# Perceiver block on one core: tokens split by context quarter, output weights in the key weights' buffer, last weighings in four banks

## What is computed

```python
x = x + xattn(layernorm(x), ctx)      # q = x Wq; k, v = ctx Wk, ctx Wv
                                      # softmax(q k / sqrt(32)) v, then @ Wp + bp
x = x + attn(layernorm(x))            # q, k, v, o with biases, per-head bias on the keys
x = x + ffn(layernorm(x))             # relu(x W_fc)^2 W_proj, five spiking steps, mean of spikes
```

## Time and profile before

| | us |
|---|---|
| median of 3 runs (lowest, highest) | 1918.98 (1917.98, 1925.94) |
| the profiled execution | 1919.2 |
| its span | 1917.4 |
| PE busy in the span | 1849.8 (96%) |
| DVE, POOL, ACT busy | 1116.4, 873.9, 834.6 |
| mean granted PE clock | 0.987 of 2.4 GHz |

### The profile page before, as it was taken

One profiled execution on the slowest core, in us unless ns is written; L12 is line 12 of the kernel. 1 busy time (PEld: TensorE's weight loads), 2 busy tenths in 40 slices (PEclk: granted clock), 3 DMA queues, 4 the chain that ended last, 5 costly groups with the idle time before them and its releaser, 6 DMA issues. The chain is left out here.

```text
span 1917.4 us, 65530 instructions
## 1 busy us (share of the span) xinstructions
PE 1849.8 (96%) x28992; PEld 1595.3 (83%) x28992; DVE 1116.4 (58%) x1354; ACT 834.6 (44%) x1032; POOL 873.9 (46%) x830
## 2 busy tenths in 40 slices
PE   6999999999999999999999999999999989789998
PEld 3979898989888888888888989898989768667887
DVE  4475665657474848384848474747475561763265
ACT  4444444545453535353535353545444413334322
POOL 0293636454554546372728282828272620544211
PEclk9999999999999999999999999999999989789999
DMA  5200202011010202020202020202020140222110
GB/s 211 85 4 3 76 3 76 16 64 45 34 68 12 77 2 77 3 77 3 76 3 76 3 76 3 76 3 76 3 75 3 67 133 23 46 72 91 52 56 23
DMA packets 38829, 94.54 MB, mean 49 GB/s; under 512 B 18593, under 2 KB 18593, under 8 KB 38305
## 3 DMA queue, kind: packets, MB, share of 16 engines
q1 hardware_dynamic: 38560, 90.26, 13.3%
HBM read 81.99 MB, written 6.16 MB: 46 GB/s over the span
## 5 line engine op out<-in xcount | busy, mean ns | idle before, releaser
L379 POOL TENSOR_TENSOR fold<-fold,prob 128x256 f32<-128x256 f32 (+1 forms) x704 | 700.3, 995 | 55.2
L98 PE MATMUL ring<-y_parts,wk_s 128*128 128x402 f32 (+1 forms) x3072 | 607.4, 351 | 1.4 <-PEq L152 1.4
L98 PE MATMUL ring<-wv_s,y_parts 128*128 128x512 f32 (+1 forms) x2496 | 596.2, 396 | 0.0
L98 PEld LDWEIGHTS ring<-y_parts,wk_s 128*128 128x128 f32 x3072 | 551.1, 188 | 17.4 <-issue 4.1
L98 PEld LDWEIGHTS ring<-wv_s,y_parts 128*128 128x128 f32 (+1 forms) x2496 | 453.8, 184 | 112.6
L373 POOL TENSOR_TENSOR fold<-prob 128x256 f32<-128x256 f32 x64 | 68.2, 1066 | 698.0 <-ACT prob L416 698.0
L393 ACT ACTIVATE k_sb<-ring 128x402 f32<-128x402 f32 (+1 forms) x256 | 129.4, 505 | 372.5 <-PE ring L98 372.5
L525 DVE TENSOR_TENSOR prob<-prob,peak_rows 128x1024 f32<-128x1024 f32 (+1 forms) x192 | 277.9, 1499 | 12.2 <-ACT peak_rows L412 12.2
L406 ACT ACTIVATE prob<-s_ps 128x1536 f32<-128x1536 f32 (+1 forms) x128 | 199.9, 1561 | 128.0 <-PE s_ps L642 128.0
L416 ACT ACTIVATE prob<-prob 128x1024 f32<-128x1024 f32 (+1 forms) x192 | 207.5, 1123 | 3.2 <-DVE prob L525 1.3
L502 DVE TENSOR_TENSOR fold<-prob 128x512 f32<-128x512 f32 x64 | 51.8, 809 | 228.2 <-ACT prob L406 228.2
(11 more groups left out here) (142 smaller groups left out, 1474.7 us busy)
## 6 DMA issues: line engine op xcount, KB each, us to landing
y_raw<-yT SPq DMA_DIRECT2D x48, 804.0 KB, 5.8
y_raw<-yT SPq DMA_DIRECT2D x16, 792.0 KB, 9.9
f_raw<-w_ffn SPq DMA_DIRECT2D x22, 512.0 KB, 3.2
p_x<-x SPq DMA_DIRECT2D x2, 1024.0 KB, 7.2
q_scratch<-p_x SPq DMA_DIRECT2D x4, 512.0 KB, 2.7
q_sb<-q_scratch SPq DMA_DIRECT2D x16, 128.0 KB, 8.5
x_sb<-x SPq DMA_DIRECT2D x4, 512.0 KB, 6.1
v_sw<-y_raw SPq DMA_DIRECT2D x4, 512.0 KB, 8.5
```

The lines of the kernel that those rows point to most:

```text
L98: mm = pe.matmul(out, left(a, c), right(b, c), start=(c == 0 and n == 0), stop=(c == DC - 1 and n == 2))
L379: pool.tensor_tensor(acc[0:m], acc[0:m], prob[0:m, i, t, :], ALU.add).then_inc(sum_step, 1)
```

## The change

Four things at the end of cross-attention, and what follows from them in later blocks:

- The parts of the attended tokens are no longer packed over the whole context (`att`) but lie as whole tiles of 128 inside the context's quarters: tiles 0 to 2 at column 0, 3 to 5 at 402, 6 and 7 at 804 (`outputs`, `attended`). So a quarter can be written once the value tiles that read it are done. The stored tokens return in three transfers, and `gather(q)` splits them, on ACT and DVE, inside the last batch's values phase.
- The parts of Wp go to `w_keep`, which is also the key weights' buffer `wk_s` (their last use is before the last values), and now stays for the whole kernel; Wo goes there later too.
- The four last weighings have a bank each: the three of the ring and `small_ps`; PE no longer waits between them. The reciprocals go to four slices of `q_sb`.
- The next block's weights lie in free columns of the context (`w_side`) instead of `awq_s` and `att_room`; `pT` of self-attention lies in `w_raw`; the feed-forward stage has 5 places of its own for weights instead of 7, and two in `w_keep` (`place_of`).

```diff
+TILES = KW // P
+BY_QUARTER = [q * KW for q in range(-(-TT // TILES))]
+TILES_LEFT = TT - TILES * (len(BY_QUARTER) - 1)
...
+        self.keep = ctx.enter_context(nc.sbuf_tensor("w_keep", [P, 2, DC, D], F32R))
-        self.w_out = parts[:, :, DC * TOK:DC * TOK + DC * D].rearrange("p s (c e) -> p s c e", c=DC)
+        side = BY_QUARTER[-1] + TILES_LEFT * P
+        self.w_side = [self.parts[:, :, :, at:at + D] for at in (side, 0, D)]
+    def outputs(self, s, q):
+        return self.parts[:, s, :, BY_QUARTER[q]:BY_QUARTER[q] + tiles_of(q) * P]
+    def attended(self, s, c, t):
+        at = BY_QUARTER[t // TILES] + t % TILES * P
+        return self.parts[:, s, c, at:at + P]
...
-        self.wk_s, self.wv_s = sb("wk_s", [P, 2, DC, D], F32R), sb("wv_s", [P, 2, DC, D], F32R)
+        self.wk_s, self.wv_s = context.keep, sb("wv_s", [P, 2, DC, D], F32R)
...
+        def last_bank(i):
+            return ring[i] if i < RING else small_ps
...
-            sp.dma_start(o_raw[:, :, 0:STORED], o_dram).then_inc(o_back, 16)
+            for q in range(len(BY_QUARTER)):
+                at = stored(q)
+                sp.dma_start(o_raw[:, :, at], o_dram[:, :, at]).then_inc(o_back[q], 16)
...
         @block.scalar
...
+            def gather(q):
+                act.wait_ge(o_back[q], 16)
+                act.wait_ge(full, UNITS * (B - 1) + KEYS + LAST_V[q] + 1)
+                act.activation(stored_part(0, q), o_raw[:, :, stored(q)], ACT.Copy).then_inc(out_hi, 1)
...
                 value(b, 3)
                 if more:
                     high(b + 1, 0)
+                else:
+                    act.wait_ge(wp_in, 16)
+                    act.activation(y.keep[:, 0], y.w_raw, ACT.Copy).then_inc(wp_hi, 1)
                 value(b, 5)
                 peak_row(b, 3)
                 if more:
                     high(b + 1, 1)
+                else:
+                    gather(0)
...
-            act.wait_ge(full, UNITS * B)
-            act.wait_ge(wp_in, 16)
-            act.activation(y.w_out[:, 0], y.w_raw, ACT.Copy).then_inc(out_hi, 1)
-            act.wait_ge(o_back, 16)
-            for c in range(DC):
-                act.activation(y.att[:, 0, c, 0:STORED], o_raw[:, c, 0:STORED], ACT.Copy).then_inc(out_hi, 1)
             act.wait_ge(o_out, NBLK * B)
-            act.activation(y.att[:, 0, :, STORED:TOK], o_sb[:], ACT.Copy).then_inc(out_hi, 1)
+            act.activation(last_part(0), o_sb[:], ACT.Copy).then_inc(out_hi, 1)
...
         @block.vector
...
+            def gather(q):
+                dve.wait_ge(out_hi, q + 1)
+                dve.tensor_tensor(stored_part(1, q), o_raw[:, :, stored(q)], stored_part(0, q).bitcast(F32),
+                                  ALU.subtract)
...
-            dve.wait_ge(out_hi, 1)
-            dve.tensor_tensor(y.w_out[:, 1], y.w_raw, y.w_out[:, 0].bitcast(F32), ALU.subtract)
-            output(B - 1, 0)
-            output(B - 1, 1)
-            output(B - 1, 2)
-            output(B - 1, 3)
-            for c in range(DC):
-                dve.wait_ge(out_hi, 2 + c)
-                dve.tensor_tensor(y.att[:, 1, c, 0:STORED], o_raw[:, c, 0:STORED],
-                                  y.att[:, 0, c, 0:STORED].bitcast(F32), ALU.subtract)
+            output(B - 1, 0, last_bank(0), q_sb[:, 0, :])
+            gather(2)
+            output(B - 1, 1, last_bank(1), q_sb[:, 1, :])
+            output(B - 1, 2, last_bank(2), q_sb[:, 2, :])
+            output(B - 1, 3, last_bank(3), q_sb[:, 3, :])
...
             for i in range(NBLK):
-                if i:
-                    small_output(B - 1, i - 1)
-                weigh(B - 1, i)
+                weigh(B - 1, i, last_bank(i))
...
-    RAW, OWN, HELD, AS, HS, HB = 3, 7, 13, 2, 3, 4
+    RAW, OWN, HELD, AS, HS, HB = 3, 5, 13, 2, 3, 4
+    FREE = OWN + 2
```

More of the change, by code:

```diff
@@ L107, in reached, with tiles_of @@
     eng.wait_ge(sem, count)
+TILES = KW // P
+BY_QUARTER = [q * KW for q in range(-(-TT // TILES))]
+TILES_LEFT = TT - TILES * (len(BY_QUARTER) - 1)
+def tiles_of(q):
+    return TILES if q < len(BY_QUARTER) - 1 else TILES_LEFT
 class Context:
@@ L330, in row, with stored, stored_part, last_part @@
             return peak_rows[:].unsqueeze(1).broadcast_to((P, b - a, HQ))
+        def stored(q):
+            return slice(q * TILES * P, min(q * TILES * P + tiles_of(q) * P, STORED))
+        def stored_part(s, q):
+            return y.outputs(s, q)[:, :, 0:stored(q).stop - stored(q).start]
+        def last_part(s):
+            return y.outputs(s, len(BY_QUARTER) - 1)[:, :, -N:]
         def half_tiles(h):
@@ L462, in values_phase @@
                     high(b + 1, 2)
+                else:
+                    gather(1)
                 value(b, 11)
@@ L525, in subtract, with output @@
                     dve.tensor_tensor(piece(i, n), piece(i, n), row(n), ALU.subtract).then_inc(sub_ok, 1)
[L527 removed]
+            def output(b, i, at=small_ps, share=rec[:]):
                 block = NBLK * b + i
                 dve.wait_ge(pv_ok, block + 1)
[L530 removed]
+                dve.reciprocal(share, at[:, N:2 * N]).then_inc(rec_ok, 1)
                 dve.wait_ge(rec_ok, block + 1)
@@ L571, in values_phase @@
                     low(b + 1, 1)
+                else:
+                    dve.wait_ge(wp_hi, 1)
+                    dve.tensor_tensor(y.keep[:, 1], y.w_raw, y.keep[:, 0].bitcast(F32), ALU.subtract)
                 value(b, 10)
@@ L848, in output_and_qkv @@
         bp_sb, bv_sb, b_col = sb("bp_sb", [P, D]), sb("bv_sb", [P, D]), sb("b_col", [P, 2, NBLK])
-        wq_s = sb("awq_s", [P, 2, DC, D], F32R)
         w_qk = sb("aw_raw", [P, 2, DC, D])
         w_raw = [w_qk[:, 0], w_qk[:, 1], context.w_raw]
-        att_room = [context.att[:, a].rearrange("p c t -> p (c t)").rearrange("p (s c e) -> p s c e", s=2, c=DC)
-                    for a in range(2)]
-        w_s = [wq_s[:], *att_room]
+        w_s = context.w_side
         bank = [ctx.enter_context(nc.psum_tensor(f"co_ps{i}", [P, 512], F32)) for i in range(8)]
-        norm = OutputAndNorm(nc, ctx, "co", context.att, context.w_out, x_sb, xnT, context.rows, ident, bank)
+        norm = OutputAndNorm(nc, ctx, "co", context.attended, context.keep, x_sb, xnT, context.rows, ident, bank)
         x_in, bp_in, b_in, bv_in = [sem(f"x_in{n}") for n in range(4)], sem("bp_in"), sem("b_in"), sem("bv_in")
@@ L914, in _ @@
             act.wait_ge(wo_in, 16)
-            act.activation(context.w_out[:, 0], context.w_raw, ACT.Copy).then_inc(wo_hi, 1)
+            act.activation(context.keep[:, 0], context.w_raw, ACT.Copy).then_inc(wo_hi, 1)
         @block.vector
@@ L940, in _ @@
                     dve.wait_ge(wo_hi, 1)
-                    dve.tensor_tensor(context.w_out[:, 1], context.w_raw, context.w_out[:, 0].bitcast(F32),
+                    dve.tensor_tensor(context.keep[:, 1], context.w_raw, context.keep[:, 0].bitcast(F32),
                                       ALU.subtract)
@@ L1178, in output_and_feed_forward @@
         h_ps, y_ps = bank[:4], bank[4:]
-        norm = OutputAndNorm(nc, ctx, "so", context.att, context.w_out, x_sb, xnT, context.rows, ident, bank)
+        norm = OutputAndNorm(nc, ctx, "so", lambda a, c, t: context.att[:, a, c, t * P:(t + 1) * P], context.keep, x_sb, xnT, context.rows, ident, bank)
         y_sb = context.rows.rearrange("p (t d) -> p t d", t=TT)
@@ L1200, in place_of @@
         def place_of(load):
-            if load % HELD < OWN:
-                return w_own[:, load % HELD]
-            at = (load % HELD - OWN) * 2 * D
-            return context.parts[:].rearrange("p s c m -> p s (c m)")[:, :, at:at + 2 * D]
+            slot = load % HELD
+            if slot < OWN:
+                return w_own[:, slot]
+            if slot < OWN + 6:
+                at = (DC * TOK + (slot - OWN) * 2 * D) % (6 * 2 * D)
+                return context.parts[:].rearrange("p s c m -> p s (c m)")[:, :, at:at + 2 * D]
+            at = (slot - OWN - 6) * 2 * D
+            return context.keep[:].rearrange("p s c e -> p s (c e)")[:, :, at:at + 2 * D]
         def tokens(n):
```

29 lines of the change are left out of this document (15 added, 14 removed).

## The result

| | before | with the change |
|---|---|---|
| median of 9 runs (lowest, highest), us | 1921.0 (1917.09, 1925.94) | 1913.74 (1911.41, 1916.78) |
| the profiled execution, us | 1919.2 | 1911.55 |
| its span, us | 1917.4 | 1909.4 |
| PE busy, us | 1849.8 | 1846.3 |
| mean granted PE clock | 0.987 | 0.989 |

The account below looks back on a forecast made before the run. PE, 96% busy, was taken as the bound, waiting for DVE around the last weighings. 10.5 us (4.1 waits, 2.7 clock, 3.7 tail) plus 1.5 at the next stage made 12.0 off 1919.2: 1907.2 us, range 1903.0 to 1913.5.

Parts of the forecast that it names:

- Weighings in four banks: End of cross-attention: PE's three waits for DVE vanish, fourth weighing ends at 1533.80 us; 4.1 us from waits, 2.7 from clock.
- Full clock in the weighings: Last four weighings: PE's granted clock stays full, worth 2.7 us on the second and third.
- Rival (2): Last weighings run at half clock: 1914.6 us, or 1911.6 with two of four at half speed; chance 0.12.
- The tail: From the fourth weighing's end to the next stage's first product: 2.10 us, a gain of 3.7 us.
- The range: Whole kernel: 1903.0 to 1913.5 us, from gains of 12.4 and 7.6 us with 3 and 2 us of luck.
- The splits beside the values at no cost: Value phase: ACT's and DVE's moved splits fit into gaps ahead of value copies, nothing late; tight ACT gap 0.9 us spare.
- Rivals (3): Value phase: the five split pieces each delay PE by 0.5 us, giving back 2.5 us, 1909.7 us; chance 0.09.
- (4): Value phase: ACT waits for the first quarter's transfer; slower by over 0.5% from a landing at 1532.2; chance 0.02.
- The next stage's start: First 72 products after cross-attention: shorter gap helps the clock; gain 1.0 to 1.9 us, middle 1.5 taken.
- the upper case: Next stage's start: clock stays at 1.00, products end 2.6 us earlier, but DVE limits the gain to 1.9 us.
- The sum of 12.4: Whole kernel's gain in us if the shortened gap keeps full clock into the next stage: 10.5 + 1.9, 1906.8 us.
- Everything else at nothing: Rest of the kernel: three transfers land in time, moved buffers change only addresses; no cost or gain.

Follow-up runs that it names:

- banks alone: The kernel before with a bank for each of the four last weighings, splits still behind the value products; ratio 0.997 to the kernel before.
- the weighings doubled: The changed kernel with the 52 products of each of the last four weighings done twice; 1926.33 us, ratio 1.0024 to the kernel before.
- the splits alone: The changed kernel with the last weighings in one bank again, splits still moved into the value phase; ratio 0.9962 to the kernel before.
- the weighings put between: The changed kernel with the last batch's weighings cut up between value products 7 to 12; ratio 0.9929 to the kernel before, 1911.01 us in the second set.

## Why the prediction was wrong

- **The step that failed** is "1526.93 + 3 x 1.70 + 1.77 = 1533.80 us for the end of the fourth" under *Weighings in four banks*. The 1.70 us was measured on one weighing between large products, where instructions come in while the large ones run. Four in a row took 9.67 us, 2.8 more than the 6.87 of the sum. In its place the runs showed a limit that the sum did not have: PE used up its instructions faster than they came. With banks alone the 2.8 us are there, half of it while no other engine works; with the weighings doubled the stops follow the count of instructions; spread out, they vanish. The waits that the banks removed had been covering part of it, about half by the run with the splits alone.
- **Full clock in the weighings** was right: no row of them is at 0.50. Rival (2), slow weighings, had the direction and a time near the measured one (1911.6 to 1914.6) by a cause that did not occur.
- **The tail** was right to 0.01 us: 2.09 against 2.10. **The range** has a slip of its own: 1919.2 less 12.4 and 3 is 1903.8, not 1903.0. It does not touch the miss, which is at the other end.
- **The splits beside the values at no cost** held: PE's value products run without a stop, and from ACT's peak row to the first weighing it takes 17.61 us as against 17.60 before. Rivals (3) and (4) did not occur; the pieces of the stored tokens landed 8.0 and 9.1 us after their issue. A bound on the way was broken: POOL's totals grew by 5.5 us, not at most the 4.0 of DVE's two-input work. The 4.0 had counted two of DVE's three pieces. By the prediction's own times the third, at 1526.65, began before the bound of 1527.5 and had to be counted; and two of them were longer than worked out. Beside the totals DVE did 2.76 + 1.88 + 1.75 = 6.4 us of it. The totals still ended (1528.6) well before the fourth weighing needed them.
- **The next stage's start** was forecast with 1.5 us between 1.0 and 1.9; 1.03 came. The clock stayed at 1.00 after the gap of 2.09 us, the upper case; the product stretch shrank from 19.51 to 16.90 as worked out, and DVE added the fourth tile at 1550.24, 11.9 us after the stage's first product instead of 14.1. What was gained on the clock was then given back to DVE's small operations: 2.02 us for a pair that had taken 0.36, while the one ahead of it went only from 0.95 to 0.44. That the shorter gap keeps the clock, as the prediction read the Trainium skill ("TensorE: Matmul & The Clock Gate", Part 1), agrees with this run but not with the splits alone, where the clock fell after 2.10 us. The prediction was right not to rely on it. The sum of 12.4 did not come out, for the other reasons.
- **Behind the stage**, 9.09 us of lead became 7.37 by the end of self-attention and 8.0 at the end of the span. The prediction had put 2 to 3 us of luck there, and *Everything else at nothing* for the buffers that moved. Luck alone is doubtful: from the first scores to the feed-forward stage's first product the two traces with the old placement (before, banks alone) take 44.4 and 45.5 us at a mean granted clock of 0.77 and 0.74, and the seven with the new one 45.9 to 46.9 us at 0.59 to 0.71. Nine single traces are not a proof, and no experiment separates the placement from the clock, so its cost of perhaps 1 to 2 us is not shown.

In numbers: 10.5 forecast to the next stage, 7.7 measured (2.8 missing, supply), with 0.35 of lead from before it; 1.5 forecast there, 1.0 measured; 1.1 lost later. Together 8.0 in the span, 7.65 in the profiled executions, 7.3 in the medians.

## What to carry to other kernels

A duration read between large instructions is not the rate of a run of small ones: before waits between bursts of small matrix products are removed, count the instructions, products and weight loads (a product can be two records of each), and set them against what the trace shows of the supply, here blocks of 256 in 3.5 to 3.75 us. Where the supply comes short, spread the small products between large ones (as value products here) rather than give them more banks. And work that is ready should not stand behind work that is not: moving the splits out of the tail alone gave 5.9 of the 7.7 us up to the next stage.

## What the runs showed that was not expected

- PE stopped for 0.95 to 1.75 us with all its semaphores reached, after every 128 small product records with their 128 weight loads: twice with the change and with the banks alone, six times with the weighings doubled. With waits between the weighings one stop of 0.91 us was left. Nothing in the rows names it but "issue" and the instruction queue's packets.
- After gaps of 2.09 and 2.10 us the clock stayed at 1.00 with the change and fell to 0.50 with the splits alone.
- Beside two-input operations of DVE, POOL's eleven additions went from 8.88 to 14.39 us, 5.5 more beside 6.4 us of such work, while DVE's split of the output weights went from 2.29 to 2.76 us. One of POOL's additions, 0.74 us in the median, took 2.88. With the weighings put between, where one split of 2.28 us ran beside them, they took 10.99 us, 2.1 more.
- DVE's first small operations of the stage behind cross-attention take 0.8 to 1.9 us more than the same ones later, in every trace here.
